# Last expert stage of a graph network layer: where the last gather goes, when bias times gate is formed, and when two index columns are written

## The reference, cut to what matters

```python
logits = xf @ Wg.T + bg                         # xf: 1250 x 768, after a layernorm
probs = softmax(logits)
top2_vals, top2_idx = top_k(probs, 2)           # cw holds the two gates of each row, zero elsewhere
h = gelu(einsum('nd,edh->neh', xf, W1) + b1)    # 8 experts, 768 -> 384
y = einsum('neh,ehd->ned', h, W2) + b2          # 384 -> 768
x = x + einsum('ne,ned->nd', cw, y)
```

## Time and profile before

| | us |
|---|---|
| median of 3 runs | 1891.58 |
| the runs | 1890.46 to 1893.55 |
| the profiled execution, time | 1887.73 |
| the profiled execution, span from the first to the last instruction | 1885.8 |

### The profile page before, as it was taken

One profiled execution on the slowest core, in us unless ns is written; L12 is line 12 of the kernel. 1 busy time (PEld: TensorE's weight loads), 2 busy tenths in 40 slices (PEclk: granted clock), 3 DMA queues, 4 the chain that ended last, 5 costly groups with the idle time before them and its releaser, 6 DMA issues.

```text
span 1885.8 us, 24720 instructions
## 1 busy us (share of the span) xinstructions
PE 1766.0 (94%) x7994; PEld 1089.7 (58%) x7995; DVE 724.2 (38%) x1827; ACT 392.3 (21%) x1034; POOL 131.8 (7%) x170
## 2 busy tenths in 40 slices
PE   7999999999999985999978999999999999689996
PEld 4555555654333343566657855555579569556664
DVE  4321545756789997111116211151111114522221
ACT  2441231103322222111113321000221221122221
POOL 0000000000000001111124000000000000013222
PEclk9999999999999997899998999999999999889999
DMA  6002100001001114345546011010010012535773
GB/s 196 1 0 71 59 26 37 1 1 43 22 28 43 33 42 192 113 174 198 194 141 180 21 47 50 0 51 0 0 51 1 0 59 90 216 78 148 204 190 61
DMA packets 53662, 144.40 MB, mean 77 GB/s; under 512 B 9806, under 2 KB 20450, under 8 KB 53125
## 3 DMA queue, kind: packets, MB, share of 16 engines
q1 hardware_dynamic: 34053, 87.05, 13.3%
q0 software_dynamic: 12032, 36.23, 7.9%
q10 hardware_dynamic: 7488, 19.93, 3.0%
HBM read 114.08 MB, written 33.99 MB: 79 GB/s over the span
## 4 chain that ended last, share of the span: by engine, by line
PE 85%; DVE 8%; issue 2%; DVEq 2%; DMA 2%; ACT 1%; ACTq 0%; POOL 0%; SPq 0%; POOLq 0%
PE PS L730 21%; PE PS L1072 10%; PE PS L740 8%; PE PS L1182 5%; PE PS L1204 5%; PE PS L838 4%; PE PS L1113 4%; PE PS L872 4%; PE PS L1154 4%; PE PS L1140 4%; DVE WRA L1863 3%; PE PS L978 3%; PE PS L819 2%; PE PS L1050 2%; PE PS L987 2%
## 5 line engine op out<-in xcount | busy, mean ns | idle before, releaser
L730 PE MATMUL PS<-WS,XT 128*125 128x384 f32 x960 | 312.4, 487 | 1.4 <-issue 1.4
L730 PEld LDWEIGHTS PS<-WS,XT 128*125 128x125 f32 x960 | 179.9, 188 | 128.9 <-issue 2.6
L1072 PE MATMUL PS<-WS,XGT 128*128 x600 | 199.3, 489 | 0.0
L1072 PEld LDWEIGHTS PS<-WS,XGT 128*128 128x128 f32 x600 | 113.0, 192 | 74.3 <-issue 1.9
L740 PE MATMUL PS<-XT,WS 128*128 128x416 f32 (+1 forms) x432 | 151.2, 512 | 0.0
L1863 DVE SCALAR_TENSOR_TENSOR WRA<-RB,U,AT 125x500 f32<-125x500 f32 (+1 forms) x240 | 140.0, 647 | 2.2 <-PE PS L987 0.6
L1997 DVE TENSOR_TENSOR YS<-PS,EBB 128x768 f32<-128x768 f32 x48 | 46.0, 958 | 244.4 <-PE PS L1072 191.2
L740 PEld LDWEIGHTS PS<-XT,WS 128*128 128x128 f32 x432 | 81.6, 189 | 69.2 <-issue 69.2
L978 PE MATMUL PS<-WRA,F 125*64 125x500 f32 (+1 forms) x480 | 100.0, 527 | 9.9 <-DVE WRA L1863 8.8
L621 POOL DMA_INDIRECT XG<-xn_rows,IDX x53 | 52.1, 983 | 749.9 <-DVEq L1958 643.5
L1182 PE MATMUL PS<-WS,XGT 128*128 x288 | 99.5, 496 | 1.1 <-ACTq L1402 1.1
(11 more groups left out here) (316 smaller groups left out, 2100.2 us busy)
## 6 DMA issues: line engine op xcount, KB each, us to landing
WS<-in_ewT SPq DMA_DIRECT2D x8, 2304.0 KB, 10.7
WS<-in_fW SPq DMA_DIRECT2D x16, 1152.0 KB, 7.1
WS<-in_w SPq DMA_DIRECT2D x5, 2304.0 KB, 10.3
expert_rows<-YS ACTq DMA_DIRECT2D x25, 384.0 KB, 2.3
xn_rows<-XN ACTq DMA_DIRECT2D x20, 336.0 KB
RB<-expert_rows SPq DMA_DIRECT2D x12, 488.3 KB
WS<-in_wp SPq DMA_DIRECT2D x2, 2304.0 KB, 8.3
WS<-in_W SPq DMA_DIRECT2D x2, 2304.0 KB, 8.6
```

The lines of the kernel that those rows point to most:

```text
L730: last = nc.tensor.matmul(ps[0:T, 0:HC], lhsT[:, k, t * T:(t + 1) * T], w[:, k, b * HC:(b + 1) * HC], start=(k == 0), stop=(k == KC - 1))
L1072: last = nc.tensor.matmul(PS[:, 4 + 2 * a + b, 0:HC], XGT[:, a, k, :], WS[:, bass.ds(slot, 1), k * C + b * HC:k * C + (b + 1) * HC].rearra ...
```

## The change

There are three edits, all in the second layer's experts. The last loop no longer gathers behind its last tile, and the waits that counted that gather are lowered. `expert_rows` forms bias times gate in `YS` ahead of the wait for the second product, and then adds gate times product in one instruction; the destinations' column is copied ahead of it too. The wait for the earlier adding transfer out of this half of `YS` stands ahead of that first multiplication. At the stage's start the index columns of the third and fourth tile (tiles 2 and 3) are written ahead of the first bias. Columns from tile 4 on come from `SIDX` instead of `TOK`, and all gathers of this stage have a bounds check. The diff:

```diff
         def fetch(L, b):
-            nc.gpsimd.indirect_dma_start(out=XG[:, b, :], out_offset=None, in_=xn_d,
-                                         in_offset=bass.IndirectOffsetOnAxis(ap=IDX[:, b:b + 1], axis=0)
-                                         ).then_inc(xg_in[L][b], 16)
+            if L == 1:
+                nc.gpsimd.indirect_dma_start(out=XG[:, b, :], out_offset=None, in_=xn_d,
+                                             in_offset=bass.IndirectOffsetOnAxis(ap=IDX[:, b:b + 1], axis=0)
+                                             ).then_inc(xg_in[L][b], 16)
+            else:
+                nc.gpsimd.indirect_dma_start(out=XG[:, b, :], out_offset=None, in_=xn_d,
+                                             in_offset=bass.IndirectOffsetOnAxis(ap=IDX[:, b:b + 1], axis=0),
+                                             bounds_check=N - 1, oob_is_err=False).then_inc(xg_in[L][b], 16)
...
         with nc.gpsimd.Fori(0, over) as j:
             add_rows(n * 2 + j + 4, 0, [(1, n + 2), (0, n + j + 2)])
-            gather3(n * 2 + j + 6, 0)
...
-        pool.wait_ge(xg_in[3][0], (n + over) * 16 + 64)
+        pool.wait_ge(xg_in[3][0], n * 16 + 64)
...
-            turn(3, n + 1, 0, (turns3 + j) * 16 + 32, copied=n + 3)
+            turn(3, n + 1, 0, turns3 * 16 + 32, copied=n + 3)
...
         def expert_rows(L, n, a, i):
             b0 = 4 + 2 * a if L == 1 else 5
             e = nc.vector.value_load(TAB[0:1, 0, bass.ds(n, 1)], min_val=0, max_val=NE - 1)
+            if L == 3:
+                gate = GTE[:, bass.ds(n, 1)]
+                if not isinstance(i, int):
+                    dve.wait_ge(ys_out[L][a], i * 16)
+                V.tensor_scalar(YS[:, a, :], EBB[L][:, bass.ds(e, 1), :].rearrange("p a c -> p (a c)"), gate, None, ALU.mult)
+                V.tensor_copy(SX[:, a:a + 1], SIDX[:, bass.ds(n, 1)])
+                V.drain()
+                dve.wait_ge(y_filled[L], n + 2)
+                ys = YS[:, a, :].rearrange("p (b c) -> p b c", b=2)
+                V.scalar_tensor_tensor(out=ys, in0=PS[:, b0:b0 + 2, 0:HC], scalar=gate, in1=ys, op0=ALU.mult,
+                                       op1=ALU.add).then_inc(y_free[L], 1)
+                V.drain().then_inc(ys_ready, 1)
+                return
             dve.wait_ge(y_filled[L], n + 2)
-            if L == 1:
-                dve.wait_ge(ys_out[L][a], i * 16 + 16)
-            elif not isinstance(i, int):
-                dve.wait_ge(ys_out[L][a], i * 16)
+            dve.wait_ge(ys_out[L][a], i * 16 + 16)
             V.tensor_tensor(YS[:, a, :].rearrange("p (b c) -> p b c", b=2), PS[:, b0:b0 + 2, 0:HC],
                             EBB[L][:, bass.ds(e, 1), :].rearrange("p a (b c) -> p (a b) c", b=2), ALU.add).then_inc(y_free[L], 1)
-            if L == 3:
-                V.tensor_copy(SX[:, a:a + 1], SIDX[:, bass.ds(n, 1)])
-                V.drain()
-                V.tensor_scalar(YS[:, a, :], YS[:, a, :], GTE[:, bass.ds(n, 1)], None, ALU.mult).then_inc(ys_ready, 1)
...
-        def row_index(m, b, turned):
+        def row_index(m, b, turned, rows=SIDX):
             dve.wait_ge(turned_n[3], turned)
-            V.tensor_copy(IDX[:, b:b + 1], TOK[:, bass.ds(m, 1)]).then_inc(idx_ready, 1)
+            V.tensor_copy(IDX[:, b:b + 1], rows[:, bass.ds(m, 1)]).then_inc(idx_ready, 1)

         V.drain().then_inc(hid_summed[3], 1)
+        row_index(2, 0, 2, TOK)
+        row_index(3, 1, 3, TOK)
         hidden_bias(0, 0)
-        row_index(2, 0, 2)
-        row_index(3, 1, 3)
...
             expert_rows(3, n, 0, turns3 + j)
             hidden_bias(n + 1, 0, turned=n + 2)
-            row_index(n + 2, 0, n + 4)
```

## The result

The changed kernel takes 1882.15 us at the median of 5 runs (1880.52 to 1883.25), the kernel before 1891.58 (1888.66 to 1894.15, 5 runs). The ratio is 0.9949, with a 95% interval of 0.9938 to 0.9960: 9.6 us less, 7.6 to 11.7. The forecast was 1882.5.

What follows compares the result with a forecast made beforehand. PE was taken to bound the last stage's steady stretch, leaving time only at its start and end. +0.60 - 3.69 - 2.46 - 3.5 = -9.05 us took 1891.58 to 1882.5, range 1880.0 to 1886.8.

Steps and rivals of the forecast that it cites:

- likeliest case: The forecast itself: 1882.5 us at the median, with its own range from 1881 to 1884.5; chance 0.53.
- sum of 9.05: Whole kernel: +0.60 - 3.69 - 2.46 - 3.5 = -9.05 us, for the bounds check, gap, clock and end.
- The gap, -3.69: Last stage's start: PE's idle wait for tile 2's gather goes, with its index column written earlier; -3.69 us.
- The clock, -2.46: Behind that gap: tile 2's transposes and the following product run at full instead of mostly half clock; 0.88 + 1.58 us gained.
- The first rival: Stage's start: the clock falls all the same, or rises later behind a later first gather; sum -6.6, 1885.0 us; chance 0.17.
- The bounds check, +0.60: Every gather of the stage gets dearer, only the first on the path: +0.60 us, bounds 0 and 1.74.
- The gate's order: Per tile behind the second product: `ys_ready` comes 0.71 us earlier by one combined instruction; buys nothing in 22 of 23 tiles.
- The contention with POOL: End phase: tile 22's DVE multiplication beside tile 21's transfer may cost POOL up to about 0.8 us; kept in the range.
- The end, -3.5: Kernel's end: without the last gather the closing drain starts at 1877.0 instead of 1880.5; -3.5 us.
- The drain, 5.06: POOL's closing drain at the kernel's end: assumed to keep its 5.06 us; its length was called the unknown.
- The second rival: Kernel's end: the closing drain decides and moves with the adding transfer alone, 0.7 instead of 3.5; 1885.3 us; chance 0.13.
- the third: Kernel's end: the closing drain shrinks to 0.36 us without a gather just ahead; sum -13.8, 1877.8 us; chance 0.06.

## Why the prediction was right, and where it was not

The forecast of 1882.5 stands beside 1882.15, and its likeliest case is the one that came. That the two agree to 0.35 us is partly luck. The profiled execution was forecast at 1878.7 and took 1882.65, and 3.6 us of that difference arose ahead of the stage, in code that the change leaves alone. In it start and end are 4.75 and 3.91 us shorter, 8.66 together, against a sum of 9.05. The low bound of the range, 1880.0, is 0.4 us below what its own terms give (1882.5 - 0.6 - 1.5). By its steps:

- **The gap, -3.69.** Right: no idle PE between `turn_hidden(0)` and `turn(2)`. What is late next was seen only in part: beside the gelu there is a stall of 0.33 us between the transposes of tile 2 and the product behind them.
- **The clock, -2.46.** Right in kind. The product takes 4.13 us instead of the forecast 3.87, since it starts after a stall. With the 0.33 the two unforeseen pieces are 0.6 us. Filling the gap shortened the start by 2.0 us with the gather as late as before, which shows the part by itself. The first rival's first half, that the clock falls all the same, did not come in any of the eight profiles with the columns ahead: tile 2's transposes take 0.66 us in each. Its second half, a clock that rises later, came once (see below).
- **The bounds check, +0.60.** The term that was mis-sized: 0.05 us. I took the whole difference to an adding transfer; nearly all of that belongs to something else in which the two differ, the adding or the direction, which no run separates. Chance cancelled it against the 0.6 us of the line above: the start was forecast 5.55 us shorter and is 5.6 to 5.9 us shorter in all profiles with the columns ahead and PE's start left alone, except that of the changed kernel itself (4.75).
- **That one exception.** Tile 0's first product took 6.15 us there, against 4.75 to 5.15 in the other profiles without matmuls ahead of it. The clock rose later: the product began at 1660.15, and the granted clock is 0.50 up to 1664.0 and 1.00 from 1665.0; with the columns alone it began at 1661.79, and the clock is 1.00 from 1664.0. It cost about 1 us of the start. The edit is not the cause, since the same code with other drains does not show it. What decides it in one execution is left open. The Trainium skill, "TensorE: Matmul & The Clock Gate", section "What's actually happening", has the monitor run free of the kernel's start, which would do it; no run here tests that.
- **The gate's order.** 1.016 us for the combined instruction (forecast 1.017), 0.73 us sooner to the transfer (0.71), nothing in 22 of 23 tiles. Undoing it lengthens the end by 0.55 us.
- **The contention with POOL.** I placed the multiplication of tile 22 beside the transfer of tile 21 and kept 0.8 us for it. It came at 1863.36, inside that transfer (1863.07 to 1864.64), which took 1.57 us as before; the multiplication took its 0.62. With POOL first neither lost there. Along the stage it is the other way round, and gathers reach 1.25 us. The gather of 1851.43 had 0.32 us of the multiplication still ahead and took 1.23 us, 0.23 more than the shortest; PE's cover takes it. That agrees in direction with the rule of "SBUF — State Buffer" in the Trainium skill, section "Who interferes with whom", by which the later one waits for the end of the earlier, here 0.32 us. The 0.62 us that I priced by that rule would need both to start together.
- **The end, -3.5.** 3.9 in the profile: 3.0 for the gather (alone), some 0.6 for the order, and the rest, 0.3, has no run of its own.
- **The drain, 5.06.** The value was right and the reason was not. I took it for the closing drain's own length. It is a bill for the indirect transfers since the last drain, and the change kept it only because it removes one of 70. The second rival (it moves with the adding transfers alone) and the third (0.36 us without a gather ahead) are both out; the 0.36 of other drains was short because each had one transfer behind it, landed already, and the 3.6 at most was a wait for one in flight.
